# One ViT block with a routed FFN: the routed part with folded affine and padded tiles, and the key parts written into padded slots from two adjacent banks

## The reference

```python
p = patches16x16(x); h = ln(p)*g+b @ W + b; h = ln(h)*g+b          # embedding, 768 -> 192
a = layernorm(h); q, k, v = split(a @ w_attn + b_attn)              # attention, causal
scores = q k^T + q rel^T ; probs = softmax(causal(scores)); h = h + (probs v) @ w_proj + b_proj
z = layernorm(h); normed = ln(z)*g1 + b1                            # routed FFN
scores = sigmoid(normed @ Wr + br); idx = the 29 tokens with the lowest score
attn_out = softmax((normed Wq+bq)(normed Wk+bk)^T/4) (normed Wv+bv) @ Wo + bo   # needed for idx only
w = scores / (sum(scores) + 1e-6); pooled = sum_l w * normed
mix_out = (normed + scores * pooled) @ Wm + bm                      # for all other tokens
h2 = z + where(idx, attn_out, mix_out)
out = h2 + gelu((ln(h2)*g2+b2) @ W1 + bf1) @ W2 + bf2
```

## Time and profile before

| | us |
|---|---|
| median of 3 runs | 7143.11 (7137.82 to 7144.05) |
| profiled execution | 7138.35, span 7136.6 |
| PE busy | 6388.1 (90%) |
| PEld busy | 5565.0 (78%) |
| DVE busy | 5387.4 (75%) |
| ACT busy | 3645.2 (51%) |
| POOL busy | 3458.2 (48%) |
| PE MATMUL with `fwm` L627 waiting for `aT` | 257.2 in 126 waits |
| PE MATMUL L781 waiting for `sel` | 121.6 in 126 waits |
| PE MATMUL L619 waiting for `z` | 107.2 in 128 waits |
| PE MATMUL L714 waiting for `y_row` | 101.8 in 127 waits |

### The profile page before, as it was taken

How to read it: one execution, slowest core, us unless ns; L and a number is a source line. 1 busy time by engine, 2 the same in 40 slices (tenths; PEclk the granted TensorE clock), 3 DMA queues, 4 the chain that set the end, 5 groups by cost and what they waited for, 6 DMA issues and landing times.

```text
span 7136.6 us, 158568 instructions
## 1 busy us (share of the span) xinstructions
PE 6388.1 (90%) x51392; PEld 5565.0 (78%) x51392; DVE 5387.4 (75%) x15934; ACT 3645.2 (51%) x12160; POOL 3458.2 (48%) x4559
## 2 busy tenths in 40 slices
PE   4999999999999999999999999999999999999998
PEld 4777777777777777777777777777777777777777
DVE  3777777777777777777777777777777777777776
ACT  1555555554555555555555554555555555555554
POOL 4444444445444444444444445444444444444443
PEclk8888888888888888888888888888888888888887
DMA  4211121112112111211121112112111211121110
GB/s 47 30 22 23 22 29 22 23 25 27 23 22 27 24 23 22 29 22 23 22 29 22 23 25 27 23 22 27 24 23 22 29 22 23 22 29 22 23 25 8
DMA packets 228657, 175.82 MB, mean 25 GB/s; under 512 B 27785, under 2 KB 228126, under 8 KB 228630
## 3 DMA queue, kind: packets, MB, share of 16 engines
q1 hardware_dynamic: 218934, 173.46, 18.6%
q10 hardware_dynamic: 8336, 1.07, 0.2%
q0 software_dynamic: 1360, 0.96, 0.2%
HBM read 156.11 MB, written 19.27 MB: 25 GB/s over the span
## 4 chain that ended last, share of the span: by engine, by line
issue 28%; PE 21%; POOL 19%; DVE 18%; POOLq 9%; DVEq 3%; ACT 1%; ACTq 0%
POOL p L503 10%; PE bank L693 8%; DVE qz L1109 5%; POOL rstd L486 4%; PE bank L645 4%; DVE negmax L1128 2%; DVE z L1062 2%; PE bank L681 2%; POOLq L556 2%; POOL h L557 2%; POOLq L485 2%; PE bank L781 2%; POOL res L565 2%; PE bank L792 2%; POOLq L582 2%
## 5 line engine op out<-in xcount | busy, mean ns | idle before, releaser
L1514 ACT ACTIVATE p<-bank,negmax 98x98 f32<-98x98 f32 (+1 forms) x3072 | 1132.9, 376 | 318.8 <-DVE negmax L1128 275.8
L503 POOL TENSOR_TENSOR p<-p,rden 98x294 f32<-98x294 f32 (+1 forms) x1024 | 947.4, 950 | 610.9 <-DVE rden L1142 610.9
L1522 ACT COPY pT<-bank 98x392 f32<-98x392 f32 x768 | 374.2, 488 | 1304.4 <-PE bank L714 1297.4
L693 PE MATMUL bank<-tokw,x_sb 128*98 128x193 f32 x4096 | 988.4, 403 | 9.1 <-DVEq L1049 9.1
L693 PEld LDWEIGHTS bank<-tokw,x_sb 128*98 128x98 f32 x4096 | 874.4, 263 | 80.6 <-issue 29.2
L1128 DVE TENSOR_REDUCE negmax<-bank 98x1 f32<-98x196 f32 (+2 forms) x1536 | 627.3, 457 | 324.4 <-PE bank L681 324.2
L714 PE MATMUL bank<-ident,p 98*98 98x98 f32 x4608 | 727.8, 319 | 106.2 <-DVE y_row L1161 101.8
L714 PEld LDWEIGHTS bank<-ident,p 98*98 98x98 f32 x4608 | 561.8, 166 | 283.8 <-issue 140.4
L681 PE MATMUL bank<-qk_parts,qz 128*98 128x196 f32 (+1 forms) x6144 | 744.8, 266 | 0.0
L681 PEld LDWEIGHTS bank<-qk_parts,qz 128*98 128x98 f32 x6144 | 657.0, 166 | 11.4
L520 POOL TENSOR_TENSOR qz<-qk_parts,ones 32x588 fp32r<-32x588 f32 x256 | 301.1, 1176 | 722.1 <-DVE qk_parts L1099 701.8
(11 more groups left out here) (271 smaller groups left out, 15081.2 us busy)
## 6 DMA issues: line engine op xcount, KB each, us to landing
x_sb<-in_x SPq DMA_DIRECT2D x384, 196.0 KB, 4.8
x_sb<-in_x SPq DMA_DIRECT2D x384, 189.0 KB, 7.9
out<-out_row SPq DMA_DIRECT2D x128, 147.0 KB
x_store<-in_L_tok_W SPq DMA_DIRECT2D x6, 96.0 KB
stage<-in_L_ffn_W SPq DMA_DIRECT2D x1, 576.0 KB
gstore<-in_L_ffn_W SPq DMA_DIRECT2D x1, 384.0 KB
p<-in_L_attn_w_attn ACTq DMA_DIRECT2D x2, 96.0 KB
gstore<-in_L_ffn_W ACTq DMA_DIRECT2D x1, 192.0 KB
```

What stands on the lines that cost most here:

```text
L503: last = gp.tensor_tensor(heads, heads, rden[:, s, t].unsqueeze(2).broadcast_to([HT, NG, w]), ALU.mult)
L693: mm(bank[b][0:HT, t * (D + 1):(t + 1) * (D + 1)], xf[:, a:a + (HT - 1) * PS + 1:PS], tokw[:, q], start=t == 0 and q == 0, stop=q == QH - ...
L1514: sc.activation((p1 if t else p0)[0:HT, 3 * s + g], bank[b][0:HT, c0:c0 + (T if t else HT)], ACT.Exp, bias=negmax[:, s, t, g:g + 1], accum ...
L1522: sc.copy(pt_dst(name[0], int(name[1:])), bank[RING[name]][0:HT, 0:4 * HT]).then_inc(sem["pT_act"], 1)
```

## The change

- The gain g1 is multiplied into the weights `fwk`, `fwv`, `fwm`, `wr` and `fwq` once, ahead of the loop, and b1's share goes into the biases. The transposed z0 is split straight from PSUM (`cols_hi`, `cols_lo`), as the other operands are; `nT` goes.
- The router's scores are made in 98 rows, the sigmoid of a token's own score only (98 x 2). Ranking compares twice instead of four times.
- The mixing is reordered: `normed @ Wm` is made first (`mixing_rows`, into bank 4, between S2 and the gather), the weighted sum of these rows by two matmuls (`weighted_sum`), and `mix` on VectorE adds the two. `mix`'s result goes to GpSimd, which adds the bias, masks and adds f0. The late split and the late matmuls with `fwm` go.
- f0 is made by ScalarE at the end of the pass (`block_input`), with `shift` from GpSimd.
- Score units are by group: for g = 0..2 one unit of 4 blocks of 98 x 98 and two of 2 blocks of 98 x 196, nine in all. Now the queries are used as they are (`qparts`), and the keys are written into a zeroed tile `kz` with 32 rows in use for each slot: the high part by ScalarE, the low part by VectorE, each in four instructions of 32 x 588 that read two adjacent banks at once (`grouped`). A unit is one mask and two matmuls of 392 columns. Keys are made ahead of the queries on PE, ACT and DVE.
- Normalisation is by group, three times four heads. `RING` is new.
- Padding with zeros: `bqparts` and `onesr` to 128 rows (were 64), `nsel`, `kk`, `qb1`, `fwq`, `fwo` to 128 rows, `ctxT` to 66 columns (was 32), `selT` and `ao` to 128 rows (were 29).

```diff
-RING = dict(S0=0, S1=1, S2=2, T0=3, S3=0, S4=1, S5=2, S6=0, S7=1, A0=2, A1=0, A2=3, B0=1, A3=2,
-            B1=0, A4=1, A5=3, B2=0)
+RING = dict(S0=0, S1=1, S2=2, T0=3, S3=0, S4=1, S5=2, S6=0, S7=1, S8=2, A0=0, A1=1, B0=3, A2=2,
...
+            A3=0, B1=1, A4=3, A5=2, B2=0)
...
-    s, second = divmod(u, 2)
-    if second:
-        return s, [(0, 1, 0), (1, 1, T)]
-    return s, [(2, 1, 0), (0, 0, T), (1, 0, T + HT), (2, 0, T + 2 * HT)]
+    g, part = divmod(u, 3)
+    if part:
+        return g, 1, range(2 * part - 2, 2 * part), T
+    return g, 0, range(4), HT
...
+        def grouped(b0):
+
+            return banks[:, 512 * b0:512 * b0 + 1024].rearrange("p (g w) -> p g w", w=256)[
+                :, 0:NG, 0:T]
...
-                    gp.wait_ge(sem["sel_sb"], after("sel_sb", m))
-                    gp.tensor_tensor(f1[:], both(fbm), keep[:].unsqueeze(2).broadcast_to(
+                    gp.wait_ge(sem["mixed_sb"], after("mixed_sb", m))
+                    gp.tensor_tensor(f1[:], mixed[:], both(fbm), ALU.add)
+                    gp.drain()
+                    gp.tensor_tensor(f1[:], f1[:], keep[:].unsqueeze(2).broadcast_to(
                         [HT, 2, D]), ALU.mult)
                     gp.drain()
+                    gp.wait_ge(sem["f0_sb"], after("f0_sb", m))
                     gp.tensor_tensor(f1[:], f1[:], f0[:], ALU.add).then_inc(sem["f1b_sb"], 1)
...
+                    gp.tensor_tensor(nmean[:], mv_f[:, :, 0], r, ALU.mult)
+                    gp.drain()
+                    gp.tensor_tensor(shift[:], nmean[:], neg1[:], ALU.mult).then_inc(sem["shift_sb"], 1)
...
-                    s, heads = s_unit(u)
-
-                    if u % 2:
-                        masked = bank[b][0:HT, 0:2 * T].rearrange("p (h w) -> p h w", w=T)[:, :, HT:T]
-                    else:
-                        masked = bank[b][0:HT, HT:5 * HT].rearrange("p (h w) -> p h w", w=HT)
-                    blocks = 2 if u % 2 else 4
-                    mm(masked, identh[:], tri[:].unsqueeze(1).broadcast_to([HT, blocks, HT]),
-                       start=True, stop=False, skip_group_check=True)
-                    for i, (g, t, c0) in enumerate(heads):
-                        w = T if t else HT
-                        for part in (khi, klo):
-                            last = mm(bank[b][0:HT, c0:c0 + w],
-                                      qz[:, s, g, HT * t:HT * t + HT], part[:, g, 0:w],
-                                      start=False, stop=i == len(heads) - 1 and part is klo,
-                                      skip_group_check=True)
+                    g, t, slots, w = s_unit(u)
+                    o = bank[b][0:HT, 0:w * len(slots)]
+                    masked = o.rearrange("p (s w) -> p s w", w=w)[:, :, w - HT:w]
+                    mm(masked, identh[:], tri[:].unsqueeze(1).broadcast_to(
+                        [HT, len(slots), HT]), start=True, stop=False, skip_group_check=True)
+                    for part in range(2):
+                        last = mm(o, qparts[:, g, HT * t:HT * t + HT],
+                                  kz[:, part, slots[0]:slots[-1] + 1, g, 0:w], start=False,
+                                  stop=part == 1, skip_group_check=True)
...
-                    if front:
-                        pe.wait_ge(sem["v_sb"], after("v_sb", n))
+                    pe.wait_ge(sem["mixed_sb"], after("mixed_sb", m))
                     mm(bank[5][:, 0:T], qb0[:, 0:4], kk[:, 0], start=True, stop=True)
                     mm(bank[5][:, T:2 * T], qb0[:, 4:8], kk[:, 0], start=True, stop=True)
-                    mm(bank[4][:, 0:T], qb1[:], kk[0:64, 1], start=True,
+                    mm(bank[4][:, 0:T], qb1[:], kk[:, 1], start=True,
...
+                def mixing_rows():
+
+                    if front:
+                        pe.wait_ge(sem["v_sb"], after("v_sb", n))
+                    cols_to_rows(4, nTs, split["fwm"], "mrow_mm")
+
+                def weighted_sum():
+
+                    pe.wait_ge(sem["mrow_sb"], after("mrow_sb", m))
+                    pe.wait_ge(sem["sig_sb"], after("sig_sb", m))
+                    for t in range(2):
+                        last = mm(bank[4][0:HT, 0:D + 1], sig[:, t:t + 1].broadcast_to([HT, HT]),
+                                  mrow[:, t], start=t == 0, stop=t == 1)
+                    last.then_inc(sem["usum_mm"], 1)
...
-                        last = mm(bank[6][0:SELP, 0:D], cols(ctxT, chunk), cols(fwo, chunk),
+                        last = mm(bank[6][0:66, 0:D], ctxT[:, chunk], fwo[:, chunk],
...
-                                  selT[0:NSEL, HT * t:HT * t + HT], ao[0:NSEL], start=True,
+                                  selT[:, HT * t:HT * t + HT], ao[:], start=True,
...
+                    ve.scalar_tensor_tensor(qparts, qhi.bitcast(F32), lo_rows[:], grouped(0),
+                                            ALU.mult, ALU.add).then_inc(sem["qparts_sb"], 1)
 
                 def keys():
 
                     ve.wait_ge(sem["khi_sb"], after("khi_sb", n))
-                    for b, g0, gn in ((2, 0, 2), (3, 2, 1)):
-                        last = ve.tensor_tensor(
-                            klo[:, g0:g0 + gn].rearrange("p g t -> p (g t)"), bank[b][:, 0:gn * T],
-                            khi[:, g0:g0 + gn].rearrange("p g t -> p (g t)").bitcast(F32),
-                            ALU.subtract)
+                    for s in range(4):
+                        at = slice(32 * s, 32 * s + 32)
+                        last = ve.tensor_tensor(kz[at, 1, s], grouped(2)[at],
+                                                kz[at, 0, s].bitcast(F32), ALU.subtract)
...
+                def mixing_rows():
+                    ve.wait_ge(sem["mrow_mm"], after("mrow_mm", m))
+                    ve.tensor_tensor(mrow[:, :, 0:D], rows(4), both(b1m), ALU.add).then_inc(
+                        sem["mrow_sb"], 1)
+
+                def mix():
+
+                    ve.wait_ge(sem["usum_mm"], after("usum_mm", m))
+                    ve.tensor_scalar(sse[:], bank[4][0:HT, D:D + 1], 1e-6, None, ALU.add)
                     ve.drain()
                     ve.reciprocal(rss[:], sse[:])
-
-                def mix_pooled():
-
                     ve.drain()
-                    for chunk, (lo, hi) in enumerate(KC):
-                        size = hi - lo
-                        ve.tensor_scalar(pooled[0:size, chunk:chunk + 1],
-                                         pool_raw[0:size, chunk:chunk + 1], rss[0:size], None, ALU.mult)
+                    ve.tensor_scalar(wmix[:], sig[:], rss[:], None, ALU.mult)
                     ve.drain()
-                    for chunk, (lo, hi) in enumerate(KC):
-                        size = hi - lo
-                        ve.scalar_tensor_tensor(mT[0:size, chunk], sig[0:size],
-                                                pooled[0:size, chunk:chunk + 1],
-                                                nT[0:size, chunk], ALU.mult, ALU.add)
-
-                def mix_cols():
-                    ve.drain()
-                    split_cols(mTs, mT, "mTs_sb")
+                    for t in range(2):
+                        last = ve.scalar_tensor_tensor(mixed[:, t], bank[4][0:HT, 0:D],
+                                                       wmix[:, t:t + 1], mrow[:, t, 0:D],
+                                                       ALU.mult, ALU.add)
+                    last.then_inc(sem["mixed_sb"], 1)
...
-                    maxima(3)
                     maxima(4)
                     maxima(5)
                 if back:
                     q_blocks()
-                    mix_pooled()
+                    mix()
                 if front:
                     maxima(6)
                     inverse_sums(1)
+                    maxima(7)
                 if back:
                     max2()
                 if head:
                     patch_variance()
                 if front:
-                    maxima(7)
-                    inverse_sums(2)
+                    maxima(8)
                 if head:
                     embedding()
                 if front:
+                    inverse_sums(2)
                     transposed("A0")
-                    inverse_sums(3)
-                if back:
-                    mix_cols()
+                if back:
                     context2()
                 if head:
...
-                    group_hi(khi, 2, "k_mm", "khi_sb")
+                    sc.wait_ge(sem["k_mm"], after("k_mm", n))
+                    for s in range(4):
+                        at = slice(32 * s, 32 * s + 32)
+                        last = sc.copy(kz[at, 0, s], grouped(2)[at])
+                    last.then_inc(sem["khi_sb"], 1)
...
+                def block_input():
+
+                    sc.wait_ge(sem["h2_sb"], after("h2_sb", n))
+                    sc.wait_ge(sem["shift_sb"], after("shift_sb", n))
+                    for t in range(2):
```

(12 more changed lines are left out.)

389 lines of the change are left out of this document (186 added, 203 removed).

## The result

| | before | after |
|---|---|---|
| median of the runs, us | 7141.23 (7137.82 to 7144.05, 4 runs) | 6918.78 (6907.25 to 6942.23, 4 runs) |
| ratio | | 0.9693, 95% interval 0.9666 to 0.972 |
| span of the profiled execution | 7136.6 | 6940.4 |
| mean granted clock | 0.872 | 0.892 |
| PE, DVE, ACT, POOL busy | 90, 75, 51, 48% | 85, 63, 56, 47% |

The change gains 222 us, half of the 434 that were forecast. The time lies inside the range of the prediction (6300 to 7050) and outside the narrower band of its forecast (6550 to 6860). First the list of cores of the changed kernel, then its PE timeline over one image. Its rows answer to the earlier trace rows.

What follows compares the result with a forecast made beforehand. TensorE was taken as the bound, with waits on a VectorE chain and the low clock behind them. Stretches gain 6.0 us, clock +2.5: image 54.61 to 51.1, times 126 = 441, +5 outside: 6702, median 6707; range 6300 to 7050.

Steps and rivals of the forecast that it cites:

- Start of the scores: From z0's transposes to the first score unit: scores start at 8.75 us instead of 9.08, 0.3 us gained.
- rival B's first route: 32-partition operations run slower than the slope says: +2.4 us before the scores, image 53.5, or 7005; chance 0.20 with Rival D.
- Query padding: Query matmuls: padding bqparts to 128 rows saves 1.0 us of TensorE, but the keys' chain starts the scores.
- To the gather and to S7: Gather starts at 11.3 us, 0.7 gained; S7 starts at 23.85, 1.1 gained, with a wait at scores2.
- Rival D: 392-column matmuls cost over one cycle a column: at worst 0.25 us each, 1.6 in all, image 52.7; 0.20 with B.
- A1: Second attention: TensorE stands still 3.0 us in front of A1, at t = 28.0, released by ScalarE's exponentials of S7.
- To attention times V, without clock: From S7 at 2.4 GHz: the 2.04 us aT wait goes, attention times V starts at 37.3, 2.25 us gained.
- To the next image, without clock: From attention times V to the next z0 at 2.4 GHz: 1.6 us gained, an image of 48.6.
- The clock: Low clock from A1 to the end of attention times V: between 0 and +4.0 us, +2.5 taken, image 51.1.
- A: The clock stays up: an image of 48.6 or 47.5, 6250 to 6390, up to 6540; chance 0.15.
- C: Slower: low clock through attention, projection and half of the MLP's 30 matmuls; image 55.4, 7240; chance 0.11.
- B's second route: The low clock behind A1 holds up to the projection: image 52.6, 6890; chance 0.20 with Rival D.

Runs made afterwards that it cites:

- e2: The changed kernel with 26 discarded matmuls (result never read) between A0 and A1, where TensorE stands still: 6643.99 us, ratio 0.9307.
- e4: The changed kernel with the bias operands of the queries (bqparts, onesr) 64 rows high again instead of 128: 6923.12 us, ratio 0.9696.
- e1: The changed kernel with VectorE making max2 ahead of the maxima of S7: 6704.58 us, ratio to before 0.9392.
- e10: The changed kernel with only the scatter's contracted rows (selT, ao) taken back from 128 to 29: 7133.44 us, ratio 0.9989.
- e8: The kernel before with the padding alone: ctxT 66 columns wide, fwo, selT and ao zero-padded to 128 rows: 6952.57 us, ratio 0.9736.
- e5: The changed kernel without the padding of projection and scatter (ctxT 32 columns, fwo's second chunk 64 rows, selT and ao 29 rows): 7136.08 us, ratio 0.9996.
- e12: e11 with ten more discarded matmuls ahead of z3's transposes: 6418.2 us, ratio 0.8987.
- e11: e7 with discarded matmuls in two more waits, seven ahead of the context's transposed columns and eight ahead of the output projection: 6613.9 us, ratio 0.9285.
- e3: The changed kernel with VectorE subtracting each slot's keys as soon as ScalarE has copied that slot, not all four: 6712.04 us, ratio 0.9401.
- e7: The changed kernel with the edits of e1 and e3, plus eight discarded matmuls ahead of A1 and eleven ahead of B0: 6518.44 us, ratio 0.9129.
- e9: The changed kernel with only ctxT's columns taken back from 66 to 32, the scatter's rows kept at 128: 6924.77 us, ratio 0.9698.

## Why the prediction was right and wrong, step by step

Places are counted from z0's transposes, as the prediction does. "High clock" is e2's images without any low clock (49.94 us each, with starts as in the table plus 0.3).

*Start of the scores:* 8.75 forecast, 9.20 measured. The prices were right, as the groups of the changed kernel show:

```profile
L1143 DVE TENSOR_TENSOR kz<-banks,kz 32x588 fp32r<-32x588 f32 x512 | 392.2, 766 | 439.5 <-ACT kz L1472 434.3
...
L1472 ACT CAST kz<-banks 32x588 fp32r<-32x588 f32 x512 | 328.1, 641 | 199.7 <-PE banks L669 195.2
```

0.78 and 0.65 were forecast. So rival B's first route (slow 32-partition operations) is false. The sum was wrong: by the prediction's own prices the chain is 2.6 + 4 x 0.65 + 4 x 0.78 + 0.78 = 9.1 us, and it was written as 8.7. So 0.3 us gained became 0.1 lost. Query padding: 1.0 us on TensorE, hidden, confirmed by e4. The prediction reads the rows of this padding as speaking against the rule on weight loads that it cites. The loads in e4 agree with the rule; the cost lies where the number of rows changes.

*To the gather and to S7:* 11.3 and 23.85 forecast, 11.6 and 24.0 measured; wait at `scores2` 1.1 forecast, 0.86 measured; no low clock at the patches, as forecast. Rival D is false: a unit of mask and two matmuls of 392 columns starts 0.44 us before the next, against 0.41 forecast (S7 and S8, at 3034.95, take 0.90 up to A0 at 3035.85).

*A1:* a wait of 3.0 us, released by ScalarE, at 28.0; measured 3.09 at 28.5. e1 shows the cause: with `max2` ahead of the maxima of S7, A1 starts 2.2 us earlier.

*To attention times V, without clock:* 37.3 forecast; 37.6 in e2.

*To the next image, without clock:* an image of 48.6 forecast, 49.94 in e2. Of the missing 1.3 us, 0.3 were there at attention times V. About 0.5 came between it and the MLP (5.15 us, where 4.76 less 1.4 gained and 1.25 given back make 4.6). The last 0.5 are the MLP: 7.18 us from its first matmul to the next z0 (3055.72 to 3062.90), where 6.6 had been forecast from 8.1 less "1.5 gained"; z0's wait was 0.79 of these, 0.95 went, and what is left is TensorE's own work and one wait of 0.29 us (L920 for `qk_parts`). That is the first term that was sized wrong.

*The clock:* bounds 0 and +4.0, +2.5 taken; 53.07 - 49.94 = +3.1 measured, and no kind of image in after goes beyond +3.8 (53.72). That is the second, and the reason given for leaning away from the upper end (the padded matmuls bring an earlier return) was right in kind: e10 shows it at the scatter. What the prediction missed is how much hangs on it: it credits the gain to five stretches, 6.0 us in all, and has the zeros of the scatter only as a reason for a smaller clock term. In the runs the zeros weigh most: alone, in the kernel before, they bring 188 us (e8), and the rest without them shows no gain (e5, with what is said there of its comparison with before); each image of e5 has 3.4 us more low clock than before. There the clock and the changes of row count cost 54.61 - 49.94 = 4.7 us, more than the upper bound of +4.0. That the time came into the range is in part luck: the range was wide, and the forecast held both the stretches and the zeros without telling what either is worth alone.

*Sum:* 1.3 (places) + 0.6 (clock) = 1.9 us per image, times 126 = 240, and the profiled execution took 6942 against the 6702 of the sum. The other runs were up to 35 us shorter.

*Rivals:* A (clock stays up in every image) came true only with the discarded matmuls of e12. C (the low clock runs past the projection) isn't seen in after or e5, where it ends in attention times V at the latest; e11 shows such a stretch in the MLP, by another wait. Nearest is B's second route, low clock up to the projection, 6890, which the prediction held to be less likely than its own value.

What stays open: why e3, which leaves the wait at A1 alone, shortens the low clock behind it by 3.3 us per image, and why e5 and e10 come out at the very image time of before (54.61); that the clock is in step with the image there is seen, that it sets the time isn't shown.

## What to carry to other kernels

Price every wait of TensorE twice, for itself and for the clock behind it, and look where the low stretch ends up: it costs most in front of dense work that nothing hides. Discarded matmuls in the wait are cheap to try, in all such waits together, as filling one more of them can lose (e11 against e7) until the last is filled too (e12). Compare images with the same low time before you call two edits non-additive. When a unit gets a new bank, follow what the old tenant waits for on every engine, not its length.

## What the runs showed of the hardware

- The scatter's matmuls with 128 contracted rows (99 of them zeros) instead of 29 are worth 215 us (e10's 7133 against after's 6919), for the most part by an earlier return of the clock; about 0.3 of the 1.7 us per image go with the change of row count. Padding from 32 to 66 columns in the matmuls ahead of it is worth nothing measurable (e9).
- 26 matmuls whose result nobody reads made the kernel 275 us faster (e2), ten more 196 us (e12 against e11).
- A matmul with 64 rows between ones of 128 costs 0.35 us more than one with 128 (e4: groups of 1.02 against 0.67), though its weight load takes no longer (184 against 192 ns).
- A copy or subtraction on 32 partitions that reads two adjacent PSUM banks (588 columns) costs what its columns say: 641 ns on ScalarE and 766 on VectorE, where the slopes of the earlier trace rows gave 0.65 and 0.78 us.
